# First aggregation of a graph block: GpSimd makes the one-hot tiles between its gathers, VectorE no longer makes them

## The reference

```python
Wh = h @ W + b                                  # 6250 x 64
e = leaky_relu(a_dst . Wh[row] + a_src . Wh[col])   # one number per edge and head
alpha = softmax of e over the edges of the same row
out[row] += alpha[:, head] * Wh[col]            # segment sum over the edges
```

## Time and profile before

| | us |
|---|---|
| median of 3 runs | 8672.77 |
| lowest and highest | 8672.36, 8692.10 |
| span of the profiled execution | 8581.5 |
| busy in it: PE, DVE, POOL, ACT | 5397.6, 4364.2, 3443.8, 1790.0 |

### The profile page before, as it was taken

The page is one execution under the profiler, slowest core; times in us unless marked ns, Lnnn a source line. Parts: engine busy times, 40 slices in busy tenths (PEclk is TensorE's granted clock), DMA queues, the critical chain, the costliest instruction groups (busy, mean ns, idle before and its releaser), DMA issues. The chain is left out here.

```text
span 8581.5 us, 97856 instructions
## 1 busy us (share of the span) xinstructions
PE 5397.6 (63%) x21196; PEld 3737.0 (44%) x21197; DVE 4364.2 (51%) x8953; ACT 1790.0 (21%) x4856; POOL 3443.8 (40%) x3669
## 2 busy tenths in 40 slices
PE   1545555555556555499745555556565555699999
PEld 1434444444444444266433333334343333466666
DVE  8955555555555555832544444445444444633333
ACT  6312222222222211322300000001111111243333
POOL 0145555455555544244054444445455444300000
PEclk7767777777777777699866666666666666799999
DMA  1021111111111111312543333333333333300000
GB/s 45 25 48 39 40 40 40 37 40 40 39 39 41 39 37 37 114 55 64 147 110 90 90 88 90 90 89 103 97 99 99 96 97 96 90 13 4 7 7 30
DMA packets 380651, 534.53 MB, mean 62 GB/s; under 512 B 119264, under 2 KB 240119, under 8 KB 380407
## 3 DMA queue, kind: packets, MB, share of 16 engines
q0 software_dynamic: 139648, 299.92, 14.5%
q1 hardware_dynamic: 240886, 233.29, 9.1%
HBM read 475.96 MB, written 56.96 MB: 62 GB/s over the span
## 5 line engine op out<-in xcount | busy, mean ns | idle before, releaser
L871 POOL DMA_INDIRECT got<-table,st_idx x3232 | 3066.9, 949 | 2933.8 <-DVE weighted L1012 1188.5
L946 PE MATMUL ps_sum<-weighted,hot 128*128 128x260 f32 x6464 | 2300.1, 515 | 2152.4 <-DVE acc L1020 1482.0
L946 PEld LDWEIGHTS ps_sum<-weighted,hot 128*128 128x128 f32 x6464 | 1564.4, 257 | 2770.1 <-DVE acc L1020 1571.4
L1020 DVE TENSOR_TENSOR acc<-acc,ps_sum 128x260 f32 x1664 | 707.2, 425 | 2948.3 <-DMA y_rows<-y_e,slot_home 1225.9
L1012 DVE TENSOR_TENSOR weighted<-got,ps_weight 128x2048 f32<-128x2048 f32 x404 | 921.6, 2281 | 9.2 <-issue 4.5
L904 ACT ACTIVATE ps_weight<-z 128x32 f32<-128x32 f32 x404 | 81.2, 201 | 3941.5 <-DVE z L1000 2914.3
L932 PE MATMUL ps_score<-score_split,hot_t 128*128 x3232 | 240.5, 188 | 487.7 <-issue 255.2
L3054 DVE SCALAR_TENSOR_TENSOR x_res<-ps_yf,comb,x_res 128x256 f32 x392 | 189.8, 484 | 638.8 <-PE ps_yf L2962 638.8
L932 PEld LDWEIGHTS ps_score<-score_split,hot_t 128*128 128x128 bf16 x3232 | 196.0, 104 | 711.0 <-issue 692.8
L971 DVE TENSOR_TENSOR hot<-ps_score,row_loc 128x1024 f32<-128x1024 f32 x404 | 492.0, 1218 | 6.8 <-issue 0.2
L2942 PE MATMUL ps_hf<-acc,ws_f 128*128 (+2 forms) x896 | 348.1, 542 | 6.0 <-ACTq L2989 6.0
(11 more groups left out here) (533 smaller groups left out, 7210.5 us busy)
## 6 DMA issues: line engine op xcount, KB each, us to landing
spread<-row_list SPq DMA_DIRECT2D x404, 256.0 KB
got<-table,st_idx POOLq DMA_INDIRECT x3232
gate_xin<-ball_rows SPq DMA_DIRECT2D x98, 128.0 KB
got_y_e<-y_rows SPq DMA_DIRECT2D x10, 896.0 KB
table<-row_e SPq DMA_DIRECT2D x50, 130.0 KB
ball_rows<-xt SPq DMA_DIRECT2D x10, 640.0 KB, 4.7
mix_xin<-ball_rows SPq DMA_DIRECT2D x49, 128.0 KB
xn_rows<-xs_m SPq DMA_DIRECT2D x49, 128.0 KB, 1.7
```

The lines of the kernel that those rows point to most:

```text
L871: pool.indirect_dma_start(got[:, r, k, :], None, table, bass.IndirectOffsetOnAxis(ap=st_idx[:, r, k:k + 1], axis=0))\
L946: last = nc.tensor.matmul(ps_g[:, p % 2, 0:AW], hot[:, r % 2, k, :], weighted[:, r % 2, k, :], start=(k == n * p), stop=(k == n * p + n - 1))
L1020: nc.vector.tensor_tensor(acc[:, ds(b * AW, AW)], acc[:, ds(b * AW, AW)], ps_g[:, p % 2, 0:AW], ALU.add).then_inc(added, 1)
```

## The change

For the first aggregation only (`if shared`), the one-hot tiles move from VectorE to GpSimd:

- `hot` has four slots instead of two.
- ScalarE also copies the step's eight columns of `row_loc` into a new tile `st_loc`, behind the copy of the indices, and signals `loc_staged`. Before it overwrites a slot it waits for `hot_ready` of the step four back.
- GpSimd waits for `loc_staged` as well. Behind each gather it makes one tile of 128x128: `g.iota_row` compared with the tile's column of `st_loc`. Ahead of the first of the eight it waits for `summed` of the step four back, which read the same slot of `hot`. The eighth signals `hot_ready`.
- VectorE leaves out `one_hot`, with the waits that stood ahead of it.
- TensorE reads the slot r of four instead of r of two.

```diff
+        st_loc = sb("st_loc", [P, STEP_RING, KT])
-        hot = sb("hot", [P, 2, KT, P])
+        HOT_STEPS = STEP_RING if shared else 2
+        hot = sb("hot", [P, HOT_STEPS, KT, P])
...
                 pool.wait_ge(idx_staged, j + 1)
+                if shared:
+                    pool.wait_ge(loc_staged, j + 1)
                 if not first:
                     pool.wait_ge(scaled, j - (STEP_RING - 1))
                 pool.nop(nofuse=True)
...
                         .then_inc(gathered[r], 16)
+                    if shared:
+                        if k == 0 and not first:
+                            pool.wait_ge(summed, first_entry(j - STEP_RING + 1))
+                            pool.nop(nofuse=True)
+                        last = nc.gpsimd.tensor_scalar(hot[:, r, k, :], g.iota_row[:, :],
+                                                       st_loc[:, r, k:k + 1], None, ALU.is_equal)
+                if shared:
+                    last.then_inc(hot_ready, 1)
...
                 nc.scalar.copy(st_idx[:, r, :], g.col_idx[:, ds((turn * STEP_RING + r) * KT, KT)]).then_inc(idx_staged, 1)
+                if shared:
+                    if not (isinstance(turn, int) and turn == 0):
+                        act.wait_ge(hot_ready, (turn - 1) * STEP_RING + r + 1)
+                    nc.scalar.copy(st_loc[:, r, :], g.row_loc[:, ds((turn * STEP_RING + r) * KT, KT)]).then_inc(loc_staged, 1)
...
-                        last = nc.tensor.matmul(ps_g[:, p % 2, 0:AW], hot[:, r % 2, k, :], weighted[:, r % 2, k, :],
+                        last = nc.tensor.matmul(ps_g[:, p % 2, 0:AW], hot[:, r % HOT_STEPS, k, :], weighted[:, r % 2, k, :],
...
-                    if exists(last, r, 1):
+                    if exists(last, r, 1) and not shared:
                         one_hot(*later(turn, r, 1), first and r + 1 < STEP_RING)
...
-            one_hot(0, 0, True)
+            if not shared:
+                one_hot(0, 0, True)
```

More of the change, by code:

```diff
@@ L807, in stage_aggregate @@
         high, peak = (ps_s[:, BEHIND + P + k * KT * 4:BEHIND + P + (k + 1) * KT * 4].rearrange("p (k c) -> p k c", c=4) for k in range(2))
-        idx_staged, hot_ready, hot_t_ready = sem("idx_staged"), sem("hot_ready"), sem("hot_t_ready")
+        idx_staged, loc_staged, hot_ready, hot_t_ready = sem("idx_staged"), sem("loc_staged"), sem("hot_ready"), sem("hot_t_ready")
         spread_in = [sem(f"spread_in{r}") for r in range(SPREAD_RING)]
@@ L970, in one_hot @@
                     dve.wait_ge(summed, first_entry(i - 1))
-                nc.vector.tensor_tensor(hot[:, r % 2, :, :], count_to.unsqueeze(1).to_broadcast([P, KT, P]),
+                nc.vector.tensor_tensor(hot[:, r % HOT_STEPS, :, :], count_to.unsqueeze(1).to_broadcast([P, KT, P]),
                                         g.row_loc[:, ds(i * KT, KT)].unsqueeze(2).to_broadcast([P, KT, P]),
```

## The result

The changed kernel takes 8776.56 us (median of 4 runs, 8761.38 to 8792.17), the kernel before on the same chip 8682.44 (8672.36 to 8704.0). The ratio is 1.0117, with a 95% interval of 1.0088 to 1.0145: 94 us more, where 303 were forecast. The direction was right, the size wrong.

What follows compares the result with a forecast made beforehand. Bound: some 8 us of dependent chain plus 5 to 6 us a step in which sums stand still while GpSimd issues gathers. (+2.0 - 0.5) x 202 = +303 us on 8672.8 gave 8976 us; range for 8 in 10, 8400 to 9220.

Steps and rivals of the forecast that it cites:

- I take 0.25 us a pair: First aggregation, GpSimd: each one-hot behind a gather lengthens the pitch from 1.25 to 1.50 us, +2.0 us a step.
- the upper bound that I gave, 0.5: GpSimd's one-hot: at most half of its 128x256 addition's median 901 ns, 0.45, with a fixed part 0.5 us.
- whatever lengthens the run lengthens it one for one: First aggregation: TensorE's sums stay held while a gather run lasts, so longer runs cost +2.0 us a step, +404 us.
- the rival of the pauses: Gathers further apart hold back fewer sums in the first aggregation; with none held -293 us, 8380 us; chance 0.18.
- GpSimd becomes the bound: From 1.83 us a pair GpSimd has no idle time left; at 1.75 us, +747 us, 9420 us; chance 0.07.
- VectorE's 0.5 us a step: First aggregation: VectorE losing its one-hot operation saves 0.5 us a step, 101 us, within bounds 0.15 and 1.13.
- The new waits at 0: GpSimd's wait for sums four steps back, and ScalarE's copy waiting for a one-hot tile, cost 0.
- that margin loses one step and stands: GpSimd's gathers work 37.8 us or 2.6 steps ahead of the weightings; one step is lost, the rest remains, cost 0.
- The wait for staged indices: GpSimd's 234.9 us wait may, with ScalarE's second copy, become 0.2 us a step, 40 us, where not covered.
- Operations that meet: GpSimd and VectorE operations locking each other out in the first aggregation: 0.2 us a step, 40 us, inside the range.
- the 91.3 us between span and median: Page's span 8581.5 against median 8672.8: taken as what lies around the profiled span, so changes were added to 8672.8.
- half relief: Half of the sums' relief from spaced gathers cancels the longer run: 8672 to 8700 us, elsewhere up to 8650.

Runs made afterwards that it cites:

- the one of 128x40: Against the kernel before: GpSimd makes a 128x40 comparison into a tile nobody reads behind each gather of the first aggregation, VectorE keeping all one-hot tiles; ratio 0.9656.
- half the tiles: Against the changed kernel: GpSimd makes four of eight one-hot tiles, behind every second gather, VectorE the other four in one operation; 8272.48 us, 0.9438 of the kernel before.
- the quarter of the tiles in the first: Against the kernel before: in the first aggregation GpSimd makes two of eight one-hot tiles, behind gathers 2 and 5, VectorE the other six; ratio 0.9410.

## Why the prediction was wrong

- **The step that failed: "I take 0.25 us a pair".** Measured 0.62 (pitch 1.87 - 1.25). It lies above the upper bound that I gave, 0.5, and above the point that I named for GpSimd becoming the bound, 1.83 us a pair. My nearest rows were the wrong kin. VectorE's comparison of 286 ns says nothing of GpSimd, where the same operation took 631 ns; GpSimd's IOTA has no input. By 128x40 in 0.41 us and 128x128 in 0.63, if the cost is a straight line through these two, a column costs 2.5 ns and the operation itself 0.31 (an estimate). The trace held one more hint that I argued down, GpSimd's addition at 715 ns and up: I halved all of it but 0.05. And I let a part of the operation hide in the gap; of that only 0.13 us did (0.30 to 0.17), while the gather beside it grew by 0.09. The estimate that the prediction made from the Trainium skill, "GPSIMD Engine Reference", 3.1 Elementwise, 0.11 to 0.19 us plus dispatch, is lower still; 2.5 ns a column, 0.32 us for 128, is above its span. Eight times that span is 0.9 to 1.5 us a step; the prediction's 1.1 to 1.8 hold a price of the dispatch for which it gives no source.
- **The other step that failed: "whatever lengthens the run lengthens it one for one".** The kernel in which VectorE makes all tiles and GpSimd compares as well, so with the longer run and nothing else changed, has no held time ahead of the adds. Measured 0 us a step where 5.2 + 2.0 were to stand. The prediction named this itself ("If that idle time shrinks with gathers further apart, the rival of the pauses is right") with a chance of 0.18, and priced it at 8380 us for a pitch of 1.5. I set it low because "0.55 is still near 0.30"; that distance was an argument and no measurement.
- **The two errors offset each other.** By the measured 0.62 with pass-through the sum is (8 x 0.62 - 0.5) x 202 = +901 us. By the measured step it is GpSimd's work, 15.26 - 14.65 = 0.61 us, x 202 = +123. Both "the pauses let the sums through" and "GpSimd becomes the bound" came true at once; I had priced the second only with pass-through added (9420), so the pair stood in none of my cases. That the kernel came out slower, as forecast, is luck: the reason given for it, sums held longer, is not what happened, and with a cheaper comparison in the same place, the one of 128x40, the kernel was faster than before (0.9656).
- **VectorE's 0.5 us a step**: 0 where GpSimd is the bound. The kernel where VectorE makes them all as well has the same step, 15.21, and at half the tiles 12.71 against 12.72.
- **The new waits at 0**: right for TensorE, in whose idle time ahead of the sums no `hot` of GpSimd's is named, only VectorE's adds and "issue". But "that margin loses one step and stands" is wrong: GpSimd has no margin left, VectorE waits 6.0 us a step for its gathers. The wait for staged indices vanished instead of growing.
- **Operations that meet**: 0.2 us a step forecast. The row of the tile view (min, median, max) is

```profile
L882 POOL TENSOR_SCALAR hot<-iota_row,st_loc x1616: 612/631/1095, 503.4 to 3583.7; 128x128 f32<-128x128 f32 x180
```

  and the mean 670 ns, so 8 x 0.04 = 0.3 us a step are such lengthening. The one at 1549.74 took 0.89 us; VectorE's `hot_t` started at 1549.75. The Trainium skill, "SBUF — State Buffer", SBUF: two separate sides, says that of such a pair the one that starts first has the port to itself and the other is shut out for a whole instruction. The trace agrees that they hinder each other, but not in this: by its rows GpSimd had started 0.01 us ahead and was the one lengthened, by 0.26 us, half of `hot_t`'s 0.49.
- **The baseline**: the 91.3 us between span and median were a quick execution or a quicker chip, not what lies around a span (1.9 us). So the +123 us by the steps holds some of that, and the 94 us of the timed runs are the better number. The first operation on `got` in the untouched second aggregation, 202 times as well, starts from 4319.8 to 7388.5 us in before and from 4453.3 to 7599.7 in the changed kernel, 15.27 and 15.65 us a step: 78 us of the 208.8 between the spans arise where nothing was changed.
- **Small slips in the working**: the case of GpSimd as the bound takes 0.3 us for VectorE's share where the sum takes 0.5 (with 0.5 it is 9380, not 9420), and half relief stands once at 8672 to 8700 and once at 8650. Neither moves the forecast.

## What to carry over

Where a queue of short transfers issued without a break stands beside another engine's completions that arrive late, try a pause first: an operation without any use, longer than the gap between two issues, gained 4.7% here in the first aggregation alone (four a step), about as much as moving half of the useful work did (5.6%), and two a step in the second, beside the quarter of the tiles in the first, took the gain from 5.9% to 12.1%. Pauses without use in both aggregations were not run. When work goes to an engine that idles, add up that engine's whole step with the new work at a price measured on that engine, and forecast the case in which it becomes the bound together with each rival, not beside them. Idle time that vanishes isn't proof that its cause has: look whether the engine now waits for something else ahead of it. And a profiled execution's span has to be held against its own run time before a term rests on it.

## What the runs showed of the hardware

- Where GpSimd has issued four or more indirect transfers 1.25 us apart, VectorE sees TensorE's sums late, up to 13 us; they came out 1.9 us behind the last transfer of a run in the three places read, whether GpSimd then waited or computed. Sums that end among the first three of a run mostly come at once. At pitches of 1.64 and 1.87 us, or 1.38 and 1.78 in turn, no sum that VectorE waited for was held. The profile models a matmul's end, so the rows don't tell a sum that is made late from one that is announced late, and what on the chip does this was not found.
- GpSimd's comparison of 128x128 with a number per partition: 0.63 us between gathers, 0.60 behind another, 0.41 for 128x40. Clearing 128x1: 0.12, 128x128 of bf16: 0.23. A gather behind one of these comparisons takes 1.03 us instead of 0.94, and the idle time ahead of it is 0.17 instead of 0.30.
